# One order for all attention rounds, and a re-planned list of side work, in a two-layer transformer kernel

## What is computed

```python
x  = L0_attn_x                       # (1, 2048, 128)
xn = _layernorm(x)
x  = x + _L0_attn_ref(xn, ...)       # 16 heads over 32 chunk means of 64 tokens ("summary attention")
       + _L0_ffn_ref(xn, ...)        # see below
xn = _layernorm(x)
x  = x + _L1_attn_ref(xn, ...)       # state-space layer, chunked scan
       + _L1_ffn_ref(xn, ...)        # 128 -> 512 -> 512 -> 512 -> 128 with GELUs
```

## Time and profile before

| what | us |
|---|---|
| median of three executions | 741.6 (740.76, 741.6, 748.94) |
| the profiled execution | 748.94 |
| its span, first to last instruction | 747.1 |
| the attention loop in it, first to last exponential | 35.2 to about 370 |

### The profile page before, as it was taken

One profiled execution on the slowest core, in us unless ns is written; L12 is line 12 of the kernel. 1 busy time (PEld: TensorE's weight loads), 2 busy tenths in 40 slices (PEclk: granted clock), 3 DMA queues, 4 the chain that ended last, 5 costly groups with the idle time before them and its releaser, 6 DMA issues.

```text
span 747.1 us, 11327 instructions
## 1 busy us (share of the span) xinstructions
PE 626.9 (84%) x4031; PEld 366.7 (49%) x4031; DVE 390.6 (52%) x986; ACT 463.7 (62%) x660; POOL 192.3 (26%) x214
## 2 busy tenths in 40 slices
PE   3398887999999999999840399819888999999997
PEld 3233224333333333333330277617775878788786
DVE  7854564212444345265359433355556667575753
ACT  2377684479999989988740144442674756557663
POOL 2094542105222042203006300063201313212231
PEclk9589887569999999999955589957898999999999
DMA  6129102001200000300160300011000000000000
GB/s 196 32 68 89 2 1 58 1 0 34 61 1 1 1 1 2 114 1 1 60 188 32 105 15 30 29 41 28 0 1 1 1 1 16 1 15 1 1 15 14
DMA packets 33428, 23.49 MB, mean 31 GB/s; under 512 B 9774, under 2 KB 27718, under 8 KB 33374
## 3 DMA queue, kind: packets, MB, share of 16 engines
q1 hardware_dynamic: 32350, 20.68, 12.8%
q0 software_dynamic: 1024, 2.10, 0.9%
HBM read 13.46 MB, written 5.39 MB: 25 GB/s over the span
## 4 chain that ended last, share of the span: by engine, by line
PE 60%; DVE 17%; ACT 9%; issue 7%; POOL 4%; DMA 2%; another core or an unknown queue 1%; DVEq 0%; ACTq 0%; POOLq 0%
PE ps L1132 17%; PE ps L1114 8%; PE ps L86 4%; PE ps L88 4%; PE ps L87 4%; POOL rows_by_expert L758 3%; PE ps L1391 2%; ACT r L838 2%; PE ps L1189 2%; PE ps L1078 2%; DVE r L2021 2%; PE ps L1178 1%; PE ps L1253 1%; DVE r L2000 1%; PE ps L1278 1%
## 5 line engine op out<-in xcount | busy, mean ns | idle before, releaser
L838 ACT ACTIVATE r<-ps 128x1024 f32<-128x1024 f32 (+3 forms) x320 | 262.8, 907 | 63.5 <-PE ps L1114 57.1
L1132 PE MATMUL ps<-r 128*32 128x512 f32 (+3 forms) x1280 | 163.1, 585 | 3.6 <-DVE r L1639 2.0
L752 POOL TENSOR_TENSOR r<-r,consts 128x256 f32<-128x256 f32 x128 | 98.8, 792 | 247.9 <-ACT r L838 247.7
L1114 PE MATMUL ps<-r2r 32*128 32x512 f32 (+3 forms) x640 | 92.6, 493 | 7.9 <-ACT r L838 6.9
L1114 PEld LDWEIGHTS ps<-r2r 32*128 32x128 f32 x640 | 39.0, 194 | 55.3 <-ACT r L838 32.6
L784 POOL TENSOR_TENSOR r<-r 128x512 f32<-128x512 f32 x16 | 23.5, 1467 | 143.2 <-ACT r L1013 114.9
L1132 PEld LDWEIGHTS ps<-r 128*32 128x32 f32 x1280 | 26.1, 111 | 41.8 <-issue 27.8
L88 PE MATMUL ps<-r2r 128*128 128x512 f32 x112 | 45.9, 410 | 0.0
L87 PE MATMUL ps<-r2r 128*128 128x512 f32 (+1 forms) x96 | 37.9, 395 | 0.0
L763 POOL DMA_INDIRECT r<-expert_rows,r x16 | 17.8, 1115 | 74.6 <-DMA expert_rows<-r 70.1
L758 POOL DMA_INDIRECT rows_by_expert<-r x16 | 19.9, 1242 | 46.3 <-DVE r L1809 41.8
(11 more groups left out here) (349 smaller groups left out, 1321.0 us busy)
## 6 DMA issues: line engine op xcount, KB each, us to landing
r2r<-r2r SPq DMA_DIRECT2D x60, 64.0 KB, 2.0
r<-in_f_W SPq DMA_DIRECT2D x1, 2048.0 KB, 8.2
rows_by_expert<-r SPq DMA_DIRECT2D x1, 1472.0 KB
expert_rows<-r SPq DMA_DIRECT2D x5, 256.0 KB, 2.2
res<-in_x SPq DMA_DIRECT2D x4, 256.0 KB, 4.2
r<-in_g_h1T SPq DMA_DIRECT2D x1, 1024.0 KB, 5.5
r<-in_g_h2T SPq DMA_DIRECT2D x1, 1024.0 KB, 8.0
r<-rows_by_expert SPq DMA_DIRECT2D x2, 512.0 KB, 4.5
```

Source lines behind the costliest of these rows:

```text
L752: pool.tensor_tensor(blk, blk, along(tri, 2), ALU.mult).then_inc(s_msk, 1)
L838: act.activation(probs[:, n % PBUFS, :, off:TB], ps[:, b:b + 2, off:TB], ACT.Exp).then_inc(s_exp, 1)
L1114: m = pe.matmul(ps[:, 2 * (n % SBUFS) + h, off:TB], kst[32 * j:32 * j + 32, g, P * kt:P * kt + P], qst[32 * j:32 * j + 32, g, qb * TB + of ...
L1132: m = pe.matmul(ps[32 * j:32 * j + 32, 6, off:TB], vp[:, kt, g, :], probs[:, (2 * v + j // 2) % PBUFS, j % 2, off:TB], start=(v == FIRST[r ...
```

## The change

All rounds, group 0 too, take their tiles in alternation. With that `KEYS_AT` becomes 17, 49 and 97. Times asked for in the plan change: KEYS(2) 34 for 34.5; QUERIES of block 2 and 3; KV is asked for at step 27 in six parts and no longer waits for KEYS(2); there is no rest behind GATE. The tanh goes one step later, the root's step follows from the plan. `spread_keys(1)` moves on SP behind the two transfers to DRAM. POOL's three weight scalings are tied to step 17. DVE's split and rotation events have simpler places.

The planner then gives: QUERIES(1,3) 29 to 30, KV 31 to 36, KEYS(2) 37, ATT(0,1) 38 to 39, GMAT 40 to 45, QUERIES(2,0) 46 to 47, G0 48 to 53; GATE at 74, 97, 122 and 166 with the tanh at 75, 98, 123 and 167 and another job (SCORE 2, SCORE 7, TRANSPOSE 10) in the step right behind each of the first three; the last OUTPUT at 151 (before: 158); the root at step 29. Its DVE order from step 30 on: QUERIES(1,3), keys_split(2), split(2), first bias addition, accumulator copy, rotated(3,0), second bias addition, KV, rotated(3,1), KEYS(2), keys_split(3), ATT(0,1).

```diff
--- before.py
+++ after.py
@@ -456,10 +456,8 @@
 
 
 
-        def key_tiles(qb, g):
+        def key_tiles(qb):
             diag, full = list(range(TPB * qb, TPB * qb + TPB)), list(range(TPB * qb))
-            if g == 0:
-                return full + diag
             order = []
             while diag or full:
                 order += full[:1] + diag[:1]
@@ -467,7 +465,7 @@
             return order
 
         BLOCKS = [(g, qb, kt, max(0, kt - TPB * qb) * P) for qb in range(NB) for g in range(NKV)
-                  for kt in key_tiles(qb, g)]
+                  for kt in key_tiles(qb)]
         STEPS = len(BLOCKS)
         of_round = lambda g, qb: [k for k, blk in enumerate(BLOCKS) if blk[:2] == (g, qb)]
         LAG = 2
@@ -487,11 +485,11 @@
         CHAIN_FROM = (64, 88, 118, 0)
         ASKED = sorted(
             [(at + 2 * n, 2, "QKV", (b, n), None, 0) for b, at in ((2, 15), (3, 20)) for n in range(2)]
-            + [(at, 1, "KEYS", b, None, 0) for b, at in ((1, 5), (2, 34.5), (3, 62))]
+            + [(at, 1, "KEYS", b, None, 0) for b, at in ((1, 5), (2, 34), (3, 62))]
             + [(3 * g - 3, 2, "QUERIES", (0, g), None, 0) for g in range(1, NKV)]
             + [(at, 2, "QUERIES", (b, g), ("KEYS", b), 1) for b, steps in
-               ((1, (13, 17, 22, 25)), (2, (34.6, 44, 58, 66)), (3, (82, 92, 107, 123))) for g, at in enumerate(steps)]
-            + [(36, 4, "KV", 0, ("KEYS", 2), 0), (35, 6, "GMAT", 0, ("KV", 0), 1), (41, 6, "G0", 0, ("KV", 0), 1),
+               ((1, (13, 17, 22, 25)), (2, (41, 44, 58, 66)), (3, (87, 99, 112, 128))) for g, at in enumerate(steps)]
+            + [(27, 6, "KV", 0, None, 0), (35, 6, "GMAT", 0, ("KV", 0), 1), (41, 6, "G0", 0, ("KV", 0), 1),
                (48, 4, "VW", 0, ("KV", 0), 1)]
             + [(LAST[r] + LAG + 1, 2, "ATT", r, None, 0) for r in PAIRED]
             + [(54 + 6 * u, 1, "SCORE", u, ("TRANSPOSE", u - 2) if u > 1 else ("VW", 0), 1) for u in range(NT)]
@@ -500,7 +498,6 @@
             + [(at, parts, what, b, (CHAIN[n - 1][0], b) if n else ("ATT", (1, b)), gap)
                for b, at in enumerate(CHAIN_FROM) for n, (what, parts, gap) in enumerate(CHAIN)],
             key=lambda e: e[0])
-        REST = {"GATE": 2}
         AUX, ended, at = [], {}, 0
         while len(AUX) < len(ASKED):
             ready = [e for e in ASKED if e[2:4] not in ended and e[0] <= at
@@ -509,7 +506,7 @@
                 _, parts, what, which, _, _ = ready[0]
                 AUX.append((range(at, at + parts), what, which))
                 ended[what, which] = at + parts - 1
-                at += parts + REST.get(what, 0)
+                at += parts
             else:
                 at += 1
         NAUX = len(AUX)
@@ -521,8 +518,8 @@
         aux_end = lambda what, which: AUX[aux_index[what, which]][0][-1]
         LAST_STEP = AUX[-1][0][-1]
         SUMM_EXP = {aux_end("SCORE", u) + 2: u for u in range(NT)}
-        TANH_AT = {aux_end('GATE', b): b for b in range(NB)}
-        ROOT_AT = 32
+        TANH_AT = {aux_end('GATE', b) + 1: b for b in range(NB)}
+        ROOT_AT = aux_end("QKV", (3, 1)) + 3
 
 
         WSPLIT = [(w1f[:, 0:2048], w1h[:, 0:2048], w1l[:, 0:2048]), (w2f, w2h, w2l),
@@ -653,13 +650,13 @@
                                      keysT[32 * g:32 * g + 32, :].bitcast(F32)).then_inc(s_krep, 16)
 
             spread_keys(0, range(1, NKV))
-            spread_keys(1)
             sp.wait_ge(s_blank, 1)
             sp.dma_start(hbuf.rearrange("(t p) d -> p t d", p=P), along(blank, SLOTS)).then_inc(s_blanked, 16)
             sp.dma_start(b1_rows.rearrange("e (c p) -> e c p", p=P),
                          io["f_b1c"].rearrange("p (e c) -> e c p", e=E), allow_slow_non_contiguous=True
                          ).then_inc(s_blanked, 16)
 
+            spread_keys(1)
             spread_keys(2)
             sp.wait_ge(s_mr, aux_index["VW", 0] + 1)
             sp.dma_start(vw_rows.rearrange("(q p) d -> p q d", p=P), vw).then_inc(s_vwr, 16)
@@ -739,7 +736,7 @@
             pool.memset(vbd[:, :, :, :], 0.0).then_inc(s_pad, 1)
             pool.wait_ge(s_pad, 2)
             for k in DIAG:
-                if k == DIAG[NKV * TPB]:
+                if k == of_round(0, 1)[1]:
                     pool.wait_ge(s_wrest, 16 * 23)
                     step.alone(pool.tensor_scalar(wo, wo, 0.5, None, ALU.mult))
                     step.alone(pool.tensor_scalar(bgc, bgc, 0.5, None, ALU.mult))
@@ -1615,19 +1612,14 @@
                 step.mark(dve.tensor_scalar(modulo, modulo, -1.0, float(E), ALU.mult, ALU.add))
                 step.settle()
 
-            keys_split_at, split_at, rotated_at = {1: 2.5, 2: ROOT_AT + 1.5}, {}, {}
-            for b in (1, 2, 3):
-                if b > 1:
-                    rotated_at[b] = max(split_at[b - 1] + 1, aux_end("QKV", (b, 1)) + 2.5)
-                if b == 3:
-                    keys_split_at[b] = max(rotated_at[b] + 2, aux_end("KEYS", 2)) + 0.6
-                split_at[b] = max(aux_end("QUERIES", (b - 1, NKV - 1)) + 0.5, keys_split_at[b] + 0.2)
+            rotated_at = lambda b: max(aux_end("QUERIES", (b - 2, NKV - 1)) + 4.5, aux_end("QKV", (b, 1)) + 2.5)
             events = sorted([(steps[-1], 3, n) for n, (steps, _, _) in enumerate(AUX)]
                             + [(LAST[r] + LAG, 1, n) for n, r in enumerate(PAIRED)]
                             + [(k + 1, 2, u) for k, u in SUMM_EXP.items()]
                             + [(aux_end("QKV", (b, 1)) + 1, 4, b) for b in (2, 3)]
-                            + [(keys_split_at[b], 4.8, b) for b in (1, 2, 3)] + [(split_at[b], 5, b) for b in (1, 2, 3)]
-                            + [(rotated_at[b] + 2 * half, 4.5, (b, half))
+                            + [(2.5, 4.8, 1), (ROOT_AT + 1.5, 4.8, 2), (max(rotated_at(3) + 2, aux_end("KEYS", 2)) + 0.5, 4.8, 3)]
+                            + [(aux_end("QUERIES", (b - 1, NKV - 1)) + 0.5, 5, b) for b in (1, 2, 3)]
+                            + [(rotated_at(b) + 2 * half, 4.5, (b, half))
                                for b in (2, 3) for half in range(2)]
                             + [(at, 6, n) for n, at in enumerate((32, 35))] + [(k, 7, b) for k, b in TANH_AT.items()]
                             + [(16.5, 8, 0), (47, 9, 0)])
```

## The result

| | before | after |
|---|---|---|
| median, us (lowest to highest) of four each on the same chip | 741.72 (740.76 to 748.94) | 751.38 (750.56 to 753.43) |
| the profiled execution | 748.94 | 754.86 |
| its span | 747.1 | 752.8 |

The ratio of after to before is 1.0156, with a 95% interval of 1.0115 to 1.0197; it is taken over executions in the faster of the two states a program shows, and is not the quotient of the medians (1.013). The kernel became slower, by 9.7 us in the medians, where 740.2 us and no change were forecast. The 751.4 lies in the range (729 to 756) and close to rival (b)'s 752, but in part by luck: between the two profiled executions a front 12 us and a back 11 us slower stand against a middle 15 us faster, and only the front is rival (b).

The account below looks back on a forecast made before the run. PE and ACT were both taken as full from 170 to 370 us, with the loop standing still before. Terms -0.9 - 2.2 + 2.75 + 1.2 - 2.25 = -1.4 us gave 741.6 - 1.4 = 740.2 us, range 729 to 756.

Parts of the forecast that it names:

- rival (b): Step 17: loop stops for block 1's keys behind the 4-byte elements, landing after about 74; 752 us, up to 760; chance 0.32.
- Steps 17 to 24: Block 1's keys: new wait of 4.9 us at step 17, loss 7.4 instead of 8.3 us; -0.9, upper bound +11.
- the queue drains at 63.4 to 65.4: Before step 17: the DRAM pair, issued 16.6 us earlier, empties its queue then, taken as 64.4; keys land at 68.4.
- 4.58 us gap: ACT idle at 78 to 83 without releaser, where the 4-byte transfer ends; supposed to vanish under the wait, otherwise add 4.6.
- Steps 25 to 55: DVE's new order: step 41 4.5 us earlier, step 56 at 167.5 instead of 169.7; -2.2 us, bounds -12 and +5.
- if the half clock again lasts to 161: Steps 41 to 56: assumed PE stays at half clock until 161, making 11.7 steps at 3.25 us.
- rival (c): Steps 25 to 55: the 41 us half-clock stretch goes; -12 in place of -2.2, 730.4 us; chance 0.24.
- Steps 56 to 158: Balance of PE and ACT: tanh waits +2.75, denser plan +1.2, alternation -2.25 us.
- The tanh: Jobs right behind three GATEs wait for it and ACT idles; +2.75 us, bounds 0 and 4.
- The denser plan: Steps 48 to 159: side work ends at step 151 instead of 158; 205.2 against 204.0 us, +1.2, bounds 0 and 3.
- The alternation: Group 0's rounds no longer end in four diagonal tiles, so ACT idles less; -2.25 us, bounds -3 and 0.
- All three signs: Wrong if keys land before 64 or after 74, first half-clock stretch is far from 41 us, or 170 to 370 moves over 4.

Follow-up runs that it names:

- e3: Kernel before with block 1's key transfers behind the two DRAM transfers, and SP waiting for that pair to land before issuing the keys; ratio to before 1.016.
- e13: Kernel before with group 0 alternating (keys wanted at step 17) and block 1's key transfers behind the DRAM pair; ratio to before 1.000.
- e14: Kernel after with the tanh back at the GATE's own step, the rest still gone; ratio to before 1.004.
- e1: Kernel before with only spread_keys(1) moved behind the two DRAM transfers, keys still wanted at step 20; ratio to before 1.002.
- e1b: Repeat of the kernel before with only spread_keys(1) moved behind the two DRAM transfers; ratio to before 1.007.
- b0: Kernel before, unchanged, run and profiled again; ratio to before 0.999.
- e8: Kernel after with the bias rows copied in whole rows of 2 KB instead of 4096 elements of 4 bytes; ratio to before 0.995.
- e15: Kernel after with the bias rows copied whole and the tanh back at the GATE's own step; 730.13 us against before's 745.56, ratio 0.980.
- e2: Kernel after with spread_keys(1) put back ahead of the two DRAM transfers; ratio to before 1.002.
- a1: Kernel after, unchanged, run and profiled again; ratio to before 1.011.
- e4: Kernel before without the two free steps behind each GATE and with the tanh one step later; ratio to before 1.008.
- e6: Kernel before with the change's early KV plan alone (KEYS(2), KV, block 2's QUERIES, root's step, DVE order); ratio to before 0.991.
- e5: Kernel before with group 0 alternating too, SP's order as before; no usable ratio, four times from 733 to 756 us.

## Why the prediction was wrong

**Steps 17 to 24, forecast -0.9, measured +11 to +12 up to step 25.** The step that failed is "the queue drains at 63.4 to 65.4", and with it "they need 0.39 x 0.63 = 0.25 us each" and "They land at 68.4". Three assumptions were in it. The queue is empty when the DMA share is: e3's share was all but gone at 62, earlier even than forecast, but the pair was reported landed only at 72.9. SP issues the keys at its old pace: it took 18 to 25 us for 16 issues, not 10. The keys were there at 75.6 (e13, e14) and at 79.3 and 79.2 (the kernel after), not 68.4. And the loop runs undisturbed until it needs the keys: where no keys are wanted before step 20, steps 9 to 16 lost 3.6, 4.4 and 9.4 us (e1, e1b, e3). That the 4.58 us gap "goes with it, under the wait" failed as well: one like it, 4.01 us, stands at 63. I had taken that gap for a part of its place; what I had seen of it (no releaser, at the end of the 4-byte transfer) pointed to a cause, and moving the cause moved the gap, though it doesn't come in every execution (b0 shows none). The bound of +11 was right, and so was the mechanism of rival (b): e13 and e14 show the wait bare, e8 and e15 show it gone. In the two executions of the kernel after, gaps of another kind (PE stood 5.5 us with no cause in the profile, ACT 4.0) came first and left 0.9 us of bare wait; but the keys landed last all the same, and with no gaps step 17 would still have stood behind them. How much of their landing at 79 and not 75.6 comes from SP's slower issues (24.6 and 24.8 us against 20.4 and 19.0) was not tested.

On the rule that the semaphore's increment is written behind all earlier writes (the Trainium skill, DMA: Bandwidth & Descriptors, Queues, rings and completion order): e13 doesn't speak against it, as its keys were reported within 2 us of the last packets of any kind. e3's 11 us between the last packets and the report agree with a report that stands behind small writes still under way, but no row shows those writes.

**Steps 25 to 55, forecast -2.2, measured -15.** The order of DVE came as added up: KV was done before KEYS(2), and no gap from 98 to 140 in the kernel after is over 3.3 us:
```profile
125.94 1.94 ACT L835 ACTIVATE r<-ps 128x1024 f32<-128x1024 f32 x2 [2.50 <-PE ps L1111]
...
134.11 1.94 ACT L835 ACTIVATE r<-ps 128x1024 f32<-128x1024 f32 x2 [3.29 <-PE ps L1111]
```
The step that failed is "if the half clock again lasts to 161". It lasted 27 us instead of 52, and PE ran at full clock from 137 on. The bound of -12, rival (c), is what happened, and it happened together with (b): I had given the two their chances as if one excluded the other. What decides the length of the stretch stays open. All kernels with 39 us and more, but for e3, have the small elements in flight from 57 to 80; all those with 24 to 31, but for e6, have them earlier or not at all. KV's place goes with it too, less closely: of the nine profiles with KV early eight have 24 to 31 us and e2 has 41; of the eleven others four have 27 to 31 and seven 39 and more. These are patterns over 20 profiles, with exceptions, and no cause that a run showed. And as the kernel before lost 52 and 55 us to it in the two executions profiled, each the longest of its set, its median execution probably loses less. The mean clocks of b0's four executions speak for it: worked out as above over the whole span, 747.03 us goes with 171 us of half clock and 737.53 with 152. So the -15 in the middle is that of two profiles, while the medians differ by +9.7.

**Steps 56 to 158, forecast +1.7, measured +8 and +11.** By terms. The tanh, forecast +2.75: ACT's idle behind it is 1.01, 1.17 and 1.07 us, 3.25 in all, which is nearly the sum that I made. The step that failed is to price the wait by ACT's idle time: PE is the fuller engine here, 197.8 of 200.4 us, and it stood 1.18, 1.92 and 2.02 us, 5.1 in all, which it can't catch up. A clock term was missing as well: of the five profiles with both the late tanh and no rest, four show half clock in the back (3.4 us in a1, e4 and e8, 10.2 in the kernel after), each time beginning 0.7 to 2.3 us behind a wait of PE, and none of the fifteen others does. Without it (e2, 205.1, against e14, 199.8) the two edits cost 5.3, close to PE's 5.1; with it 6.9 (e4 against b0) and 6.7 (a1 against e14), and 9.9 in the profiled execution of the kernel after. The bound of 4 was too low. The denser plan, forecast +1.2: 1.3 and 1.4 (e14 against e13, e6 against b0). The alternation, forecast -2.25: -1.1, of which the part in steps 48 to 55 was in my sum for this stage; I suppose that the gaps at the ends of the rounds are in part arrears of PE, which it has to work off in either order; no run tells.

**At nothing.** POOL's scalings, KEYS(3) and the weights' later start cost nothing that a stage shows: from step 159 on all kernels take 374 to 381 us.

All three signs that I had named for being wrong came: keys after 74, a long half-clock stretch of 27 us and not 41, and a back that moved by over 4 us.

## What to carry to other kernels

Before a transfer is moved in a queue, ask what it does to everybody while it is in flight, not only how long it holds those behind it; a gap without a releaser at its end can be a sign of that, and it may move along. Price a new wait on the engine that is full, not on the one whose idle time is easiest to sum. Where a change has several parts, run each alone and compare stages: here a gain in the middle was hidden under two losses, and both could be taken away with an edit of a few lines each. And where PE arrives late at a wait, the short wait doesn't clear the transfer: ask whether it could have gone on earlier.

## What the runs showed of the hardware

A copy of 16 KB in 4096 elements of 4 bytes, DRAM to DRAM, in flight for over 20 us, slowed SP's issues of other transfers from 0.63 us each to between 1.1 (e1b) and 1.55 (a1), and in ten of fifteen profiles with it ACT or DVE had waits that ended "remote". Part of such a wait can be an ordinary one: a DVE copy in the kernel after that idled 10.74 us took a product which PE ended only 1.5 us before. But in the clearest case, e5's, the results had long been there: ACT and DVE went on at 87.1 with products that PE had ended by 80.9, and from 81.4 to 87.1 none of the four computing engines did anything.
```profile
87.11 0.66 ACT L836 ACTIVATE r<-ps 128x256 f32<-128x256 f32 x2 [5.90 <-remote]
87.14 0.37 DVE L1746 RECIPROCAL r<-ps 128x16 f32<-128x16 f32 x2 [6.29 <-remote]
```
What holds the engines up, late signals or late instructions, no run tells. The size of it differed between kernels with the same instructions up to there (steps 9 to 16, with no wait for keys in them, took 16.8 and 17.6 us in e1 and e1b and 22.6 in e3, which differs only in SP's wait); why, stays open. Copied in rows of 2 KB, the same bytes show none of these waits. The landing of such a transfer was reported 11 us after the DMA engines had last been busy with it (e3). And the time at half clock in steps 25 to 55, with PE busy 39.5 us of a stretch of 41, varied from 24 to 55 us between kernels and executions, worth up to 11 us of this kernel (75.2 in e1, 86.6 in b0): no total of a single run decides here.
